# Second attention of a four-block network: the row maxima subtracted on VectorE instead of added by bf16 matmuls on TensorE

## The chip, the core and the metric

The program runs on one core of a Trainium2 chip. The metric is the device time of one execution in microseconds. The kernel before takes 2423.53 us, the median of three runs (2421.3 to 2425.45).

## What is computed

Four blocks follow each other over 2 x 1024 tokens of 256 features. The change lies in the third block's self-attention, in words "the second attention":

```python
def _attention(xq, xkv, wq, wk, wv, wo, bo):      # 16 heads of 64, both inputs are the normed x
    q = (xq @ wq).reshape(B, S, N_HEADS, D_HEAD)
    k = (xkv @ wk).reshape(B, T, N_HEADS, D_HEAD)
    v = (xkv @ wv).reshape(B, T, N_HEADS, D_HEAD)
    attn = jnp.einsum('bihd,bjhd->bhij', q, k) * D_HEAD ** (-0.5)
    attn = jax.nn.softmax(attn, axis=-1)
    out = jnp.einsum('bhij,bjhd->bihd', attn, v).reshape(B, S, D_ATTN)
    return out @ wo + bo
```

B is 2 and S and T are 1024. The softmax needs each query's largest score, which is taken off its scores before the exponential.

## The kernel before

The second attention (part_attention2, L1459 to L1838) works on 16 head pairs (PAIRS): two batches, eight pairs of heads each. TensorE, VectorE, ScalarE (ACT), GpSimd (POOL) and SP each have an instruction order written out by hand, and semaphores hold them together. Per pair there are 16 units (U): 2 halves of 512 queries times 8 blocks of 128 keys. The scores of a unit are 128 keys x 512 queries for both heads, in one of two PSUM buffers of 128x1024 (s2, named sc in the profile).

A unit n, u on TensorE (`unit`, L1594 to L1607): two bf16 matmuls (L1603) first write minus the query's maximum into the scores' buffer, from `picks`, a matrix with three rows of ones, and `shift`, which holds the negated maxima split in three bf16 parts; four fp32 matmuls (L1606; one fp32 matmul of the program appears as two instructions) then add the scores of the two heads. ScalarE takes the exponential of the whole 128x1024 from PSUM into `probs` (named pr, five buffers, KEPT; L1827). GpSimd adds the eight blocks of a half into `total` (L1686). Two units later (LAG) TensorE multiplies with the values into `o` (`values`, L1624). After each half, at units 9 and 1 of the next pair, TensorE sums `total` over the keys (`den`, L1615) into the same two buffers, ScalarE copies `o` out and inverts the sum by Ln and Exp with a table load before each (L1803, L1810, L1812), and VectorE multiplies the two (`divide`, L1738, behind the reductions of unit 3 for a pair's second half and behind unit 11's work for the first half).

The maxima of pair n+1 are found beside the units of pair n (`aside`):

- Units 0 to 2: two projections each, six in all (L1556, L1562), into `ring`, three PSUM buffers of 128x512 (ring2_, RING). ScalarE copies them out (L1791, L1796), VectorE rounds queries and keys to fp32r (L1701), two roundings each behind units 0 and 1.
- Units 3 to 10: four maxima each. TensorE computes scores of 128 queries x 512 keys in fp32r into `ring` (L1573), two before the values of that unit and two behind them; VectorE takes the row maximum of each (L1707, TENSOR_REDUCE). Maximum i waits until reduction i-3 has freed its slot.
- Unit 11: VectorE combines the halves (L1714), TensorE transposes the 16 columns of maxima (`turn`, L1578), VectorE negates and splits them in three bf16 parts (`split`, L1717 to L1731), SP writes them to DRAM (L1530) and reads them back into `shift`, three rows per head (L1536). Unit 0 of the next pair waits for it.
- Units 12 to 15 of the pairs 4, 8 and 12: two tiles of the output projection each (`project_out`, L1590), which VectorE adds to x (`add_out`, L1746).

The last pair has no successor and so only its 16 units; behind them come eight tiles of the last output projection. Before the loop, the first pair's projections, its 32 maxima and the split stand by themselves, then VectorE adds the output bias to x (`bias_out`, L1750).

Of the kernel before, what the change touches and what calls it, by code (L numbers as in the profile page):

```python
# [5 lines left out]
ALU = mybir.AluOpType  # L6
# [7 lines left out]
P = 128  # L14
# [1444 lines left out]
def part_attention2(nc, e, A):  # L1459
    with ExitStack() as ctx:  # L1460
# [14 lines left out]
        part_max, row_max = sb("pmax", [P, 2, TB, 2]), sb("rmax", [P, 2, TB])  # L1475
        top, top_rest = sb("top2", [16, P]), sb("top2_rest", [16, P])
        top_parts = [sb(f"top2_parts{i}", [16, 3, P], BF16) for i in two]
        shift = [sb(f"shift{i}", [P, T], BF16) for i in two]
        picks = sb("picks", [P, P], BF16)
# [4 lines left out]
        rows_set, shift_set = sem("rows_set2"), sem("shift_set")  # L1484
# [3 lines left out]
        top_out, shift_in = sem("top_out2"), sem("shift_in")  # L1488
        s2_made, s2_free, pv_made, sums = sem("s2m"), sem("s2f"), sem("pvm"), sem("sums")
        raw_made, rden_made, a_made, wo_made, wo_added = sem("rawm"), sem("rdenm"), sem("am"), sem("wo_made"), sem("wo_added")  # L1490
        logs = sem("logm")
        head = (slice(0, 64), slice(64, P))
# [25 lines left out]
        @block.sync  # L1518
        def _(sp):
            for i in range(1, CHUNKS):  # L1520
                for tile, src in attention2_loads(A, w[i], i):
                    sp.dma_start(tile, src).then_inc(w_in[i], 16)
            sp.dma_start(wo_w[:], A["L2_xattn_sa_wo"].rearrange("(k p) c -> p k c", p=P)).then_inc(wo_in, 16)
            sp.dma_start(wo_brep[:], A["L2_xattn_sa_bo"].partition_broadcast(P)).then_inc(wo_in, 16)
            for n, (tile, src) in enumerate(context2_loads(A, e.ctx_w0, 0)):
                sp.dma_start(tile, src).then_inc(e.ctx_w0_in[min(n, 1)], 16)
            sp.wait_ge(shift_set, 2)
            for n in range(PAIRS):
                sp.wait_ge(top_made, 5 * (n + 1))
                sp.dma_start(e.top_dram[n % 2, :, 0:16].rearrange("s r q -> r s q"), top_parts[n % 2][:]  # L1530
                             ).then_inc(top_out, 16)
                sp.wait_ge(top_out, 16 * (n + 1))
                if n >= 2:
                    sp.wait_ge(s2_made, order_of(n - 2, U - 1) + 1)
                for j in two:
                    sp.dma_start(shift[n % 2][64 * j:64 * j + 3], e.top_dram[n % 2, :, 8 * j:8 * j + 8].rearrange(  # L1536
                        "s t q -> s (t q)")).then_inc(shift_in, 16)

        @block.tensor
        def _(te):  # L1540

            def project(n, i):
# [5 lines left out]
                if i == 2 and n:  # L1548
                    te.wait_ge(top_made, 5 * (n - 1) + 1)
                if i >= RING:  # L1550
# [30 lines left out]
            def project_out(group, t):  # L1581
# [10 lines left out]
                ins.then_inc(wo_made, 1)  # L1592

            def unit(n, u):  # L1594
                half, kt = divmod(u, 8)
                at = order_of(n, u)
                if u == 0:
                    te.wait_ge(shift_in, 32 * (n + 1))
                if at >= 2:
                    te.wait_ge(s2_free, at - 1)  # L1600
                keys = slice(kt * P, (kt + 1) * P)
                for j in two:
                    te.matmul(s2[at % 2][:, j], picks[head[j]], shift[n % 2][head[j], halves[half]], start=True,  # L1603
                              stop=False)
                for j in two:
                    ins = te.matmul(s2[at % 2][:, j], kf[n % 2][head[j], keys], qf[n % 2][head[j], halves[half]],  # L1606
                                    start=False, stop=True)  # L1607
                ins.then_inc(s2_made, 1)

            def den(n, h):  # L1610
                at = den_order(n, h)
                te.wait_ge(s2_free, at - 1)
                te.wait_ge(sums, 7 * (2 * n + h + 1))
                for j in two:
                    ins = te.matmul(s2[at % 2][64 * j:64 * j + 64, 0], e.ones[:], total[h][:, j], start=True, stop=True)  # L1615
                ins.then_inc(s2_made, 1)

            def values(n, u):
                half, kt = divmod(u, 8)
                te.wait_ge(s2_free, order_of(n, u) + 1)  # L1620
                if kt == 0 and (n or half):
# [20 lines left out]
            turn(0)  # L1642
            te.wait_ge(rows_set, 2)
            te.wait_ge(shift_set, 2)
            for n in range(PAIRS):
# [23 lines left out]
        def _(pool):  # L1669
            for h in two:  # L1670
                pool.memset(shift[h][:], 0.0).then_inc(shift_set, 1)
            for n in range(PAIRS):
                for u in range(U):
# [3 lines left out]
                    at, count = U * n + u, 7 * (2 * n + half) + kt - 1  # L1677
                    pool.wait_ge(s2_free, order_of(n, u) + 1)
                    if kt == 1:
# [10 lines left out]
        def _(dve):  # L1690
            dve.memset(picks[:], 0.0).then_inc(rows_set, 1)
            dve.wait_ge(rows_set, 1)
            for j in two:
                ins = dve.memset(picks[64 * j:64 * j + 3], 1.0)
            ins.then_inc(rows_set, 1)

            def rounding(n, i):
# [18 lines left out]

            def split(n):  # L1717
                parts = top_parts[n % 2]
                dve.wait_ge(max_turned, n + 1)
                dve.tensor_scalar(top[:], ring[2][0:16, 0:P], -1.0, None, ALU.mult).then_inc(top_made, 1)  # L1720
                dve.wait_ge(top_made, 5 * n + 1)
                if n >= 2:
                    dve.wait_ge(top_out, 16 * (n - 1))
                dve.tensor_copy(parts[:, 0, :], top[:]).then_inc(top_made, 1)
                dve.wait_ge(top_made, 5 * n + 2)
                dve.tensor_tensor(out=top_rest[:], in0=top[:], in1=parts[:, 0, :], op=ALU.subtract).then_inc(top_made, 1)
                dve.wait_ge(top_made, 5 * n + 3)
                dve.tensor_copy(parts[:, 1, :], top_rest[:]).then_inc(top_made, 1)
                dve.wait_ge(top_made, 5 * n + 4)
                dve.tensor_tensor(out=parts[:, 2, :], in0=top_rest[:], in1=parts[:, 1, :],  # L1730
                                  op=ALU.subtract).then_inc(top_made, 1)  # L1731

# [25 lines left out]
            finish_maxima(0)  # L1758
            split(0)
            bias_out()  # L1760
            for n in range(PAIRS):
                for u in range(U):
                    if n + 1 < PAIRS:
                        steps, tops, turned = aside(u)
# [5 lines left out]
                        if turned:  # L1770
                            finish_maxima(n + 1)
                            split(n + 1)
                    if u == 8 + DEN_AT + 2:
# [10 lines left out]
        def _(act):  # L1784
# [20 lines left out]
            def invert(n, h):  # L1805
                at = den_order(n, h)
                act.wait_ge(s2_made, at + 1)
                if n:
                    act.wait_ge(a_made, 2 * (n - 1) + h + 1)
                act.activation(rden[h][:], s2[at % 2][:, 0], ACT.Ln).then_inc(s2_free, 1)  # L1810
                act.wait_ge(s2_free, at + 1)
                act.activation(rden[h][:], rden[h][:], ACT.Exp, scale=-1.0).then_inc(rden_made, 1)  # L1812
# [3 lines left out]
            for n in range(PAIRS):  # L1816
                for u in range(U):
                    at, here = order_of(n, u), U * n + u
                    act.wait_ge(s2_made, at + 1)
                    if here >= KEPT:  # L1820
                        act.wait_ge(pv_made, here - KEPT + 1)
                        half, kt = divmod((here - KEPT) % U, 8)
                        if kt:
                            act.wait_ge(sums, 7 * (2 * ((here - KEPT) // U) + half) + kt)
                        else:
                            act.wait_ge(sums, 7 * (2 * ((here - KEPT) // U) + half) + 1)
                    act.activation(probs[here % KEPT][:], s2[at % 2][:], ACT.Exp).then_inc(s2_free, 1)  # L1827
                    if n + 1 < PAIRS:
# [421 lines left out]
def program(nc, A, out):  # L2250
    with ExitStack() as ctx:
# [19 lines left out]
        e.mask_dram = nc.dram_tensor("mask_dram", [B, 4, T], BF16).ap()  # L2271
        e.qk_dram = nc.dram_tensor("qk_dram", [2, 8, 3, 64, T], BF16).ap()
        e.top_dram = nc.dram_tensor("top_dram", [2, 3, 32, P], BF16).ap()

# [52 lines left out]
```

## Time and profile before

| | |
|---|---|
| median of three runs | 2423.53 us |
| the profiled execution: its own time | 2423.61 us |
| the profiled execution: its span | 2421.9 us |
| mean granted TensorE clock | 0.949 of full speed |
| busy share over the span: TensorE, VectorE, ScalarE, GpSimd | 89%, 48%, 38%, 32% |
| the loop of the second attention, first to last unit | 980.5 to 1863.1 us |
| a regular pair (pair 1, from unit 12 to unit 12) | 53.5 us |

In the profile PE is TensorE's matmuls, PEld its weight loads, DVE VectorE, ACT ScalarE, POOL GpSimd, SPq SP's queue. Matmuls are pipelined: a row's duration reaches to the modelled end of the last one, so the start of the next row, not the end of the last, tells how long TensorE was taken. "x4 2.61" in a timeline is a group of four instructions that took 2.61 us from the first's start to the last's end. In square brackets stands the idle time of the engine ahead of a group and what ended it. A row of windows has the stretch, its length, the busy time of PE, PEld, DVE, ACT and POOL with their instruction counts, the granted TensorE clock, the DMA share and GB/s.

### The profile page before, as it was taken

To read this page: it belongs to the slowest core of one execution; us is meant where nothing else is said; L and a number is where in the kernel's file an instruction comes from. 1 tells how busy PE (TensorE), PEld (TensorE's weight loads), DVE (VectorE), ACT (ScalarE), POOL (GpSimd) and SP (SyncE) were. 2 spreads that over 40 slices of the span, in tenths; PEclk is the share of its full clock that TensorE was granted. 3 is DMA by queue.
4 is the path that set the end of the run, shared out by engine and by line. 5 is a ranking of instruction groups with operands and counts; after the bars stand their busy time and mean duration, and the time that the engine had idled before them with its cause. 6 is when DMAs were issued, how large, how long until landed. Compare 5 with 4: busy or idle time off the path is not lost. (4 is left out here: it accounts for less than half of the span.)

```text
span 2421.9 us, 27503 instructions
## 1 busy us (share of the span) xinstructions
PE 2144.0 (89%) x10628; PEld 1241.5 (51%) x10666; DVE 1166.1 (48%) x2077; ACT 929.9 (38%) x1413; POOL 777.5 (32%) x505
## 2 busy tenths in 40 slices
PE   5389998679889895999999999999998979898987
PEld 2234444357768683333444444333532858576766
DVE  4786662343343525645454554555451142635343
ACT  3146665223232232355535544455355321221211
POOL 3311100012131302466555664666467010202011
PEclk9699999889999996899999999999999989998989
DMA  3733420400000004000000000000000420000000
GB/s 109 110 38 40 54 29 2 109 0 1 1 1 0 1 1 119 2 1 1 1 1 1 1 1 1 1 1 1 1 1 1 121 64 1 9 1 9 0 9 9
DMA packets 48027, 51.73 MB, mean 21 GB/s; under 512 B 14618, under 2 KB 38940, under 8 KB 47620
## 3 DMA queue, kind: packets, MB, share of 16 engines
q1 hardware_dynamic: 47908, 50.12, 9.9%
q8 instruction: 77, 1.26, 0.2%
q14 instruction: 42, 0.34, 0.1%
HBM read 41.31 MB, written 8.80 MB: 21 GB/s over the span
## 5 line engine op out<-in xcount | busy, mean ns | idle before, releaser
L1686 POOL TENSOR_TENSOR total<-total,pr 128x1024 f32<-128x1024 f32 x192 | 465.0, 2422 | 242.2 <-ACT pr L1827 228.9
L1827 ACT ACTIVATE pr<-sc 128x1024 f32<-128x1024 f32 x256 | 259.7, 1021 | 355.4 <-PE sc L1606 355.4
L1707 DVE TENSOR_REDUCE pmax<-ring 128x1 f32<-128x512 f32 x512 | 325.8, 684 | 133.7 <-PE ring L1573 125.1
L1624 PE MATMUL o<-pr,v_pair 128*64 128x512 f32 x1024 | 275.7, 617 | 1.2
L1606 PE MATMUL sc<-q_full,k_full 64*128 64x512 f32 x1024 | 267.1, 591 | 0.0
L495 ACT ACTIVATE probs<-s 128x512 f32<-128x512 f32 (+1 forms) x304 | 163.2, 575 | 160.5 <-PE s L405 117.5
L1048 POOL TENSOR_TENSOR c_scores<-c_scores,c_total 128x1024 f32<-128x1024 f32 (+1 forms) x48 | 77.0, 1614 | 352.3 <-DVE c_total L1004 352.3
L1573 PE MATMUL ring<-k_round,q_round 64*128 64x512 f32 x512 | 185.2, 600 | 4.8 <-DVE pmax L1707 4.3
L973 PE MATMUL c_ps<-vw,c_pT 128*128 128x256 f32 x640 | 165.3, 418 | 22.2 <-ACT c_pT L1037 22.2
L973 PEld LDWEIGHTS c_ps<-vw,c_pT 128*128 128x128 f32 x640 | 132.2, 212 | 47.5 <-ACT c_pT L1037 25.4
L1573 PEld LDWEIGHTS ring<-k_round,q_round 64*128 64x128 f32 x512 | 74.8, 189 | 154.8 <-DVE pmax L1707 96.8
L458 DVE TENSOR_REDUCE row_max<-s 128x1 f32<-128x640 f32 (+3 forms) x128 | 126.8, 1020 | 42.7 <-PE s L387 42.3
L384 PE MATMUL s<-k_stack,q_stack 128*128 128x512 bf16 (+3 forms) x370 | 98.5, 342 | 45.3 <-DMA k_stack<-mask_dram 31.8
L923 ACT ACTIVATE c_hT<-c_ps,c_ln_b,c_ln_g 128x256 f32<-128x256 f32 x64 | 32.6, 560 | 270.1 <-PE c_ps L908 270.1
L939 PE MATMUL c_ps<-m,c_hT 128*128 128x512 f32 x256 | 121.3, 620 | 6.6 <-ACT c_hT L923 4.6
L1624 PEld LDWEIGHTS o<-pr,v_pair 128*64 128x64 f32 x1024 | 51.2, 134 | 144.2 <-issue 142.1
L1686 POOL TENSOR_TENSOR total<-pr 128x1024 f32<-128x1024 f32 x32 | 75.2, 2350 | 143.5 <-ACT pr L1827 143.5
L2121 PE MATMUL c_ps<-c_hT,hT 128*128 128x256 f32 x512 | 117.3, 392 | 4.4 <-ACT c_hT L923 4.4
L2121 PEld LDWEIGHTS c_ps<-c_hT,hT 128*128 128x128 f32 x512 | 100.2, 197 | 19.7 <-ACT c_hT L923 5.4
L1603 PE MATMUL sc<-shift,picks 64*128 64x512 bf16 x512 | 104.7, 387 | 4.8 <-DMA shift<-top_dram 4.8
L852 POOL TENSOR_TENSOR c_rstd<-c_moments,eps 128x2 f32<-128x2 f32 x48 | 9.4, 195 | 308.8 <-DVE c_moments L836 308.8
L1606 PEld LDWEIGHTS sc<-q_full,k_full 64*128 64x128 f32 x1024 | 104.5, 192 | 7.0
(278 smaller groups left out, 3407.0 us busy)
## 6 DMA issues: line engine op xcount, KB each, us to landing
qk_dram<-qk_parts SPq DMA_DIRECT2D x32, 192.0 KB, 2.8
q_stack<-qk_dram SPq DMA_DIRECT2D x48, 128.0 KB
k_stack<-qk_dram SPq DMA_DIRECT2D x48, 128.0 KB
x<-in_x SPq DMA_DIRECT2D x1, 2048.0 KB, 8.3
mlp_w<-in_L_xattn_mlp_w SPq DMA_DIRECT2D x2, 1024.0 KB, 8.4
wq<-in_L_xattn_Wq SPq DMA_DIRECT2D x2, 1024.0 KB, 6.7
wo<-in_L_xattn_Wo SPq DMA_DIRECT2D x2, 1024.0 KB, 14.9
hT<-in_L_xattn_ff_w SPq DMA_DIRECT2D x1, 2048.0 KB, 19.1
```

The source lines that it names most:

```text
L458: dve.tensor_reduce(row_max[:, heads[0], t:t + 1], src[:, 0:(t + 1) * P], AX.X, ALU.max).then_inc(s1_free, 1)
L495: act.activation(probs[at % KEPT][:, heads[0]:heads[-1] + 1, 0:width], s2[u % RING][:, 0:len(heads) * width].rearrange("p (j q) -> p j q", ...
L939: ins = te.matmul(dst, lhs[s][:, k, t * P:(t + 1) * P], m[:, s, k, c0:c0 + 512], start=k == 0, stop=k == KC - 1 and bias is None)
L973: ins = te.matmul(dst, ch.pT[s][:, c, t * P:(t + 1) * P], vw[:, s, c, :], start=c == 0, stop=c == cols // P - 1 and out_bias is None)
L1573: te.matmul(ring[i % RING][:], qr[head[j], t * P:(t + 1) * P], kr[head[j], halves[half]], start=True, stop=True).then_inc(s1_made, 1)
L1603: te.matmul(s2[at % 2][:, j], picks[head[j]], shift[n % 2][head[j], halves[half]], start=True, stop=False)
L1606: ins = te.matmul(s2[at % 2][:, j], kf[n % 2][head[j], keys], qf[n % 2][head[j], halves[half]], start=False, stop=True)
L1624: ins = te.matmul(o[64 * j:64 * j + 64], v[n % 2][:, kt, 64 * j:64 * j + 64], probs[(U * n + u) % KEPT][:, j], start=kt == 0, stop=kt == T ...
L1686: pool.tensor_tensor(out=total[half][:], in0=other[:], in1=probs[at % KEPT][:], op=ALU.add).then_inc(sums, 1)
L1707: dve.tensor_reduce(part_max[:, j, t, half:half + 1], ring[i % RING][:], AX.X, ALU.max).then_inc(s1_free, 1)
L1827: act.activation(probs[here % KEPT][:], s2[at % 2][:], ACT.Exp).then_inc(s2_free, 1)
L2121: ins = te.matmul(ch.ps[s][:, 1024 * part + 256 * f:1024 * part + 256 * (f + 1)], w.f1[:, k, chunk * P:(chunk + 1) * P], ch.hT[s][:, k, :] ...
```

## The change

VectorE now subtracts the maxima on the way out of PSUM, and TensorE adds nothing to the scores:

- The maxima stay fp32 and positive: one copy of 16x128 from PSUM (`keep_top`) takes the place of the five instructions of `split`.
- SP writes them to `level_dram` (8 KB), and one transfer sends all 8 KB to each of the 128 partitions (`level`, 128x2048 fp32, two buffers). It waits until the subtractions of the pair two before have ended.
- `unit` loses both bf16 matmuls and its wait for `shift`. It waits, as `den` does, for the step two before in the same buffers: the subtraction of a unit, or the Ln of a denominator.
- `less` is new, one per unit, 256 in all: scores (PSUM) minus `level` (SBUF) into `probs`, 128x1024 fp32. It stands first in a unit's work on VectorE, ahead of the unit's reductions and roundings, and takes over the wait for a free `probs` buffer. At unit 0 it also waits for `level`.
- The exponential runs in place in `probs`, from SBUF. GpSimd and the values wait for it by a semaphore of its own.
- `picks`, `shift` and their memsets are gone.

```diff
-            sp.wait_ge(shift_set, 2)
             for n in range(PAIRS):
-                sp.wait_ge(top_made, 5 * (n + 1))
-                sp.dma_start(e.top_dram[n % 2, :, 0:16].rearrange("s r q -> r s q"), top_parts[n % 2][:]
-                             ).then_inc(top_out, 16)
+                sp.wait_ge(top_made, n + 1)
+                sp.dma_start(e.level_dram[n % 2], top[n % 2][:]).then_inc(top_out, 16)
                 sp.wait_ge(top_out, 16 * (n + 1))
                 if n >= 2:
-                    sp.wait_ge(s2_made, order_of(n - 2, U - 1) + 1)
-                for j in two:
-                    sp.dma_start(shift[n % 2][64 * j:64 * j + 3], e.top_dram[n % 2, :, 8 * j:8 * j + 8].rearrange(
-                        "s t q -> s (t q)")).then_inc(shift_in, 16)
+                    sp.wait_ge(less_made, U * (n - 1))
+                sp.dma_start(level[n % 2][:].rearrange("p j t -> p (j t)"), e.level_dram[n % 2].rearrange(
+                    "r q -> (r q)").partition_broadcast(P)).then_inc(level_in, 16)
...
+            def slot_free(at):
+                if at >= 2:
+                    kind, n, i = turns[at - 2]
+                    if kind == "unit":
+                        te.wait_ge(less_made, U * n + i + 1)
+                    else:
+                        te.wait_ge(logs_made, 2 * n + i + 1)
+
             def unit(n, u):
                 half, kt = divmod(u, 8)
                 at = order_of(n, u)
-                if u == 0:
-                    te.wait_ge(shift_in, 32 * (n + 1))
-                if at >= 2:
-                    te.wait_ge(s2_free, at - 1)
+                slot_free(at)
                 keys = slice(kt * P, (kt + 1) * P)
                 for j in two:
-                    te.matmul(s2[at % 2][:, j], picks[head[j]], shift[n % 2][head[j], halves[half]], start=True,
-                              stop=False)
-                for j in two:
                     ins = te.matmul(s2[at % 2][:, j], kf[n % 2][head[j], keys], qf[n % 2][head[j], halves[half]],
-                                    start=False, stop=True)
+                                    start=True, stop=True)
                 ins.then_inc(s2_made, 1)
...
-            def split(n):
-                parts = top_parts[n % 2]
+            def keep_top(n):
                 dve.wait_ge(max_turned, n + 1)
...
+                dve.tensor_copy(top[n % 2][:], ring[2][0:16, 0:P]).then_inc(top_made, 1)
+
+            def less(n, u):
+                half, kt = divmod(u, 8)
+                here = U * n + u
+                dve.wait_ge(s2_made, order_of(n, u) + 1)
+                if u == 0:
+                    dve.wait_ge(level_in, 16 * (n + 1))
+                if here >= KEPT:
+                    dve.wait_ge(pv_made, here - KEPT + 1)
+                    old_half, old_kt = divmod((here - KEPT) % U, 8)
+                    dve.wait_ge(sums, 7 * (2 * ((here - KEPT) // U) + old_half) + max(old_kt, 1))
+                dve.tensor_tensor(out=probs[here % KEPT][:], in0=s2[order_of(n, u) % 2][:],
+                                  in1=level[n % 2][:, :, halves[half]], op=ALU.subtract).then_inc(less_made, 1)
...
             for n in range(PAIRS):
                 for u in range(U):
+                    less(n, u)
                     if n + 1 < PAIRS:
                         steps, tops, turned = aside(u)
...
-                    act.activation(probs[here % KEPT][:], s2[at % 2][:], ACT.Exp).then_inc(s2_free, 1)
+                    act.wait_ge(less_made, here + 1)
+                    act.activation(probs[here % KEPT][:], probs[here % KEPT][:], ACT.Exp).then_inc(exp_made, 1)
```

## Rows read from the trace of the kernel before

**Rows 1.** The page, part 1: busy time, share of the span, instructions.
```profile
PE 2144.0 (89%) x10628; PEld 1241.5 (51%) x10666; DVE 1166.1 (48%) x2077; ACT 929.9 (38%) x1413; POOL 777.5 (32%) x505
```
**Rows 2.** Windows of pair 1: units 3 to 12, then 12 to 3.
```profile
1051.07:1077.20 26.13, 25.82 (x128) 10.21 (x128) 21.61 (x34) 14.15 (x16) 17.27 (x8) 1.00 0.00 1
1077.20:1104.58 27.38, 27.29 (x125) 11.01 (x125) 7.76 (x10) 13.93 (x18) 16.58 (x8) 1.00 0.01 1
```
**Rows 3.** Timeline of TensorE in unit 6: start us, us, engine, line, what.
```profile
1060.16 0.40 PE L1603 MATMUL sc<-shift,picks 64*128 64x512 bf16 x2
1060.38 1.03 PE L1606 MATMUL sc<-q_full,k_full 64*128 64x512 f32 x4
...
1061.57 1.08 PE L1624 MATMUL o<-pr,v_pair 128*64 128x512 f32 x4
1062.58 0.49 PE L1573 MATMUL ring<-k_round,q_round 64*128 64x512 f32 x2
1062.91 0.39 PE L1603 MATMUL sc<-shift,picks 64*128 64x512 bf16 x2
```
**Rows 4.** Timeline of VectorE in the same pair: units 4 to 6, and unit 11.
```profile
1055.23 1.17 DVE L1738 TENSOR_TENSOR aT<-raw,rden 128x512 f32<-128x512 f32 x1
1056.33 3.68 DVE L1707 TENSOR_REDUCE pmax<-ring 128x1 f32<-128x512 f32 x6
...
1060.35 2.61 DVE L1707 TENSOR_REDUCE pmax<-ring 128x1 f32<-128x512 f32 x4 [0.34 <-PE ring L1573]
...
1076.32 0.17 DVE L1714 TENSOR_TENSOR rmax<-pmax 128x16 f32<-128x16 f32 x1
```
**Rows 5.** Timeline of TensorE: the transpose, unit 12, and the starts of units 14 and 15.
```profile
1076.99 0.28 PE L1578 MATMUL ring<-ident,rmax 128*16 128x128 f32 x1
1077.20 0.39 PE L1603 MATMUL sc<-shift,picks 64*128 64x512 bf16 x2
...
1081.58 0.39 PE L1603 MATMUL sc<-shift,picks 64*128 64x512 bf16 x2
...
1083.77 0.39 PE L1603 MATMUL sc<-shift,picks 64*128 64x512 bf16 x2
```
**Rows 6.** Timeline of VectorE before the loop: the first pair's maxima.
```profile
955.84 19.22 DVE L1707 TENSOR_REDUCE pmax<-ring 128x1 f32<-128x512 f32 x32 [2.94 <-PE ring L1573]
```
**Rows 7.** VectorE in a cross attention (timeline), and ScalarE's exponential from SBUF (groups).
```profile
500.60 1.22 DVE L1014 TENSOR_TENSOR c_scores<-c_ps,c_top 128x1024 f32<-128x1024 f32 x1
501.74 1.21 DVE L1001 TENSOR_REDUCE c_total<-c_scores 128x16 f32<-128x1024 f32 x1
...
L1034 ACT ACTIVATE c_scores<-c_scores 128x1024 f32<-128x1024 f32 x32 | 33.8, 1057 | 110.0 <-DVE c_scores L1014 110.0
```
**Rows 8.** Two lines of VectorE: duration in ns, min/median/max, first and last start.
```profile
L1738 DVE TENSOR_TENSOR aT<-raw,rden x32: 671/692/1177, 1028.2 to 1875.3; 128x512 f32<-128x512 f32 x32
...
L1746 DVE TENSOR_TENSOR x<-ring,x x32: 405/424/426, 1242.8 to 1891.9; 128x256 f32<-128x256 f32 x32
```
**Rows 9.** Timeline of GpSimd in the last pair.
```profile
1855.77 14.80 POOL L1686 TENSOR_TENSOR total<-total,pr 128x1024 f32<-128x1024 f32 x6 [2.49 <-ACT pr L1827]
```
**Rows 10.** Timeline of the loop's start.
```profile
977.07 4.41 DVE L1750 TENSOR_TENSOR x<-x,wo_brep 128x4096 f32<-128x4096 f32 x1
...
978.62 0.57 SPq L1536 DMA_DIRECT2D shift<-top_dram  x2
...
980.51 0.61 PE L1603 MATMUL sc<-shift,picks 64*128 64x512 bf16 x2 [4.81 <-DMA shift<-top_dram]
```
**Rows 11.** DMA issues: destination<-source, count, KB each, median us to landing.
```profile
mlp_w<-in_L_xattn_mlp_w SPq DMA_DIRECT2D x2, 1024.0 KB, 8.4
...
r_o_g<-in_L_xattn_g_out SPq DMA_DIRECT2D x1, 128.0 KB, 2.9
```
**Rows 12.** Windows before the loop, and in the first attention (columns as in rows 2).
```profile
959.00:963.00 4.00, 4.00 (x8) 1.96 (x7) 4.00 (x7) 0.00 (x0) 0.00 (x0) 0.50 1.04 214
...
145.00:150.00 5.00, 5.00 (x49) 2.87 (x47) 4.00 (x6) 3.84 (x9) 0.00 (x0) 1.00 0.02 3
```

More of the change, by code:

```diff
@@ L1475, in part_attention2 @@
         part_max, row_max = sb("pmax", [P, 2, TB, 2]), sb("rmax", [P, 2, TB])
[L1476 to L1479, printed above, removed]
+        top = [sb(f"top2_{i}", [16, P]) for i in two]
+        level = [sb(f"level{i}", [P, 2, T]) for i in two]
         ring = [ctx.enter_context(nc.psum_tensor(f"ring2_{i}", [P, 512], F32)) for i in range(RING)]
@@ L1487, in part_attention2 @@
             sem(n) for n in ("s1m", "s1f", "max_made2", "max_turned2", "top_made2"))
-        top_out, shift_in = sem("top_out2"), sem("shift_in")
-        s2_made, s2_free, pv_made, sums = sem("s2m"), sem("s2f"), sem("pvm"), sem("sums")
+        top_out, level_in = sem("top_out2"), sem("level_in")
+        s2_made, less_made, exp_made, logs_made, pv_made, sums = (
+            sem(n) for n in ("s2m", "less_made2", "exp_made2", "logs_made2", "pvm", "sums"))
         raw_made, rden_made, a_made, wo_made, wo_added = sem("rawm"), sem("rdenm"), sem("am"), sem("wo_made"), sem("wo_added")
-        logs = sem("logm")
         head = (slice(0, 64), slice(64, P))
@@ L1548, in project @@
                 if i == 2 and n:
-                    te.wait_ge(top_made, 5 * (n - 1) + 1)
+                    te.wait_ge(top_made, n)
                 if i >= RING:
@@ L1611, in den @@
                 at = den_order(n, h)
-                te.wait_ge(s2_free, at - 1)
+                slot_free(at)
                 te.wait_ge(sums, 7 * (2 * n + h + 1))
@@ L1619, in values @@
                 half, kt = divmod(u, 8)
-                te.wait_ge(s2_free, order_of(n, u) + 1)
+                te.wait_ge(exp_made, U * n + u + 1)
                 if kt == 0 and (n or half):
@@ L1669, in _ @@
         def _(pool):
-            for h in two:
-                pool.memset(shift[h][:], 0.0).then_inc(shift_set, 1)
             for n in range(PAIRS):
@@ L1690, in _ @@
         def _(dve):
[L1691 to L1695, printed above, removed]
             def rounding(n, i):
@@ L1758, in _ @@
             finish_maxima(0)
-            split(0)
+            keep_top(0)
             bias_out()
@@ L1771, in _ @@
                             finish_maxima(n + 1)
-                            split(n + 1)
+                            keep_top(n + 1)
                     if u == 8 + DEN_AT + 2:
@@ L1809, in invert @@
                     act.wait_ge(a_made, 2 * (n - 1) + h + 1)
[L1810 to L1811 removed]
+                act.activation(rden[h][:], s2[at % 2][:, 0], ACT.Ln).then_inc(logs_made, 1)
+                act.wait_ge(logs_made, 2 * n + h + 1)
                 act.activation(rden[h][:], rden[h][:], ACT.Exp, scale=-1.0).then_inc(rden_made, 1)
@@ L1817, in _ @@
                 for u in range(U):
[L1818 to L1826, printed above, removed]
-                    act.activation(probs[here % KEPT][:], s2[at % 2][:], ACT.Exp).then_inc(s2_free, 1)
+                    here = U * n + u
+                    act.wait_ge(less_made, here + 1)
+                    act.activation(probs[here % KEPT][:], probs[here % KEPT][:], ACT.Exp).then_inc(exp_made, 1)
                     if n + 1 < PAIRS:
```

16 lines of the change are left out of this document (2 added, 14 removed).

## The prediction

> **What bounds the kernel now.** I read the page's busy shares first, then windows over one head pair of the second attention, then the timelines of TensorE and VectorE inside it. On the page TensorE is busy 89% and VectorE 48% [rows 1], which looks like room for 256 new VectorE instructions; the share is a mean, so the reader should go on to the stretches. A regular pair takes 53.5 us and has two parts [rows 2]. From unit 3 to unit 12 (26.13 us, the "maxima part": eight units that carry four maxima each, then unit 11) VectorE is busy 21.61 us. From unit 12 to the next unit 3 (27.38 us, the "open part") it is busy 7.76 us. TensorE is full in both.
>
> Inside the maxima part one unit takes 1062.91 - 1060.16 = 2.75 us on TensorE, without a gap: 0.22 us from the first picks matmul to the first score matmul, 1.19 to the values, 1.01 to the last two maxima, 0.33 to the next unit [rows 3]. VectorE does four reductions in 2.61 us beside it [rows 4]. A unit of the open part that has no projection or output takes 2.19 us [rows 5]. So TensorE bounds both parts today, but in the maxima part VectorE is close behind.
>
> **How long a VectorE instruction really holds its engine.** The recorded durations overlap. Before the loop 32 reductions ran back to back in 19.22 us [rows 6]: (19.22 - 0.68)/31 = 0.598 us from start to start, while one lasts 0.68. In the loop six took 3.68 us [rows 4], again 0.60 apart. For a 128x1024 subtraction from PSUM with one operand in SBUF, the very shape of the new instruction, the trace has the cross attention's: it lasts 1.22 us and the next instruction starts 1.14 us after it [rows 7]. I take 0.60 and 1.14, which are nearest, and keep 0.68 and 1.22 as the upper end.
>
> The Trainium skill ("VectorE: DVE Perf Modes", section The DRAIN you can't avoid) says that the next instruction starts only when the pipe has emptied. Read as whole recorded durations, that gives the sum of the second case below; the rows show starts before the recorded end.
>
> **Removed: the picks matmuls.** Two per unit, 0.22 us per unit on TensorE [rows 3], 256 units: 57 us of TensorE time. This is a gain only where TensorE stays the bound. In the open part of a regular pair 7 units (12 to 15, 0 to 2) save 7 x 0.22 = 1.57 us, for 14 crossings from one pair to the next: -22 us. In the maxima part it buys nothing if VectorE is later, which is next.
>
> **Added: one subtraction per unit on VectorE, ahead of that unit's reductions.** Maxima part: 4 x 0.60 + 1.14 = 3.54 us of VectorE per unit, against 2.75 - 0.22 = 2.53 us on TensorE. The buffers don't let VectorE's work move elsewhere: the maxima have three PSUM slots, the scores two, so TensorE runs at most three reductions ahead. Is the loop longer than VectorE's own work? The fourth maximum of a unit waits for the unit's first reduction (1.14 + 0.68 = 1.82), starts some 0.06 later, the next scores 0.33 behind it, and they are there 1.08 us after (1.02 in [rows 3] and a handover): 3.3 us, before VectorE wants them at 3.54. Slack is 0.2 us. At unit 9 the denominator's matmuls use it up; I add 0.2.
>
> The part then runs: 1.1 us for unit 3's scores, 8 x 3.54 = 28.3, the division that lies at unit 3, 0.85 (1.17 there, less when GpSimd is quiet [rows 4, 8]), 0.2 at unit 9; then unit 11's subtraction, 1.14, which stands ahead of the combining of the maxima, 0.2, and the transpose, 0.21 until unit 12 [rows 4, 5] with 0.1 of handovers. Sum 32.1 against 26.13: +6.0 us. Fifteen pairs have this part (the last has no successor), the first without a division: +89 us.
>
> **Moved: the exponential now follows the subtraction.** Scores, subtraction (1.22), exponential (1.06 from SBUF [rows 7], 1.02 from PSUM today) must end before the values of two units later. In the shortest unit, 2.19 - 0.22 = 1.97 us, the values come two units and the scores' own 0.86 us (1.19 less the 0.33 of two maxima [rows 3]) after the scores' start, at 4.8 us; the chain ends at 1.1 + 1.3 + 1.1 = 3.5. Costs nothing; cover 1.3 us. On VectorE the subtraction of unit 1 stands behind the two roundings of the queries, and those behind ScalarE's copies of the projections; the order ends less than a us after today's exponential, while the values are a projection away. Nothing.
>
> **Removed: the split in three bf16 parts.** Its casts wait for GpSimd (see the division below), some 4 us per pair on VectorE, but in the open part, where VectorE has 19 us idle [rows 2]. Worth nothing in itself; GpSimd loses a disturbance.
>
> **The transfers.** Instead of two 6 KB writes SP sends the 8 KB of maxima to all 128 partitions: 1 MB. No transfer of this form is in the trace; a 128 KB broadcast landed after 2.9 us, a 1 MB load after 8.4 [rows 11]. I take 7.5 us (bounds 2.9 and, eight times a small one, 23). It is issued about 1.9 us after unit 12 and lands at 9.4; the next pair's first subtraction could run at 4 x 1.97 + 1.1 = 9.0. The 0.4 us is hidden, because TensorE has two projections next and the first thing that waits is unit 2's scores; some 3 us more would be hidden too. SP has nothing else queued there, and the buffer it writes was last read a pair earlier.
>
> **Start and end.** Today the first scores start at 980.51, held by the transfer, while VectorE adds the bias from 977.07 [rows 10]. Afterwards the scores start at once, 4.9 us earlier, but the first subtraction waits for the 1 MB, about 985. Between nothing and -5: -2.5. In the last pair the denominators wait for GpSimd, whose adds are 14.80/6 = 2.47 us apart [rows 9], more than a unit's 1.97; it starts relatively earlier, I take -2 for the whole.
>
> **Sum:** +89 - 22 - 2.5 - 2 = +62.5 us on the profiled execution's 2423.6 us, which is within 0.1 us of the median of 2423.5: 2486.
>
> **The rivals.**
> Full durations: VectorE pays 4 x 0.68 + 1.22 = 3.94 us per unit, 0.40 more, x 120 units = +48: 2533. Against it speak [rows 4, 6, 7]; for it, that no row has a reduction directly before such a subtraction with its three waits. 13%.
> Late broadcast: if it takes over some 11 us, each further us is paid at 11 crossings (the three with the output projection have 14 us more). At 15 us: +44, 2529. 3%.
> The shared path of VectorE and GpSimd: the division with both operands in SBUF lasts 671 to 1177 ns, the add with one in PSUM 405 to 426, beside the same GpSimd work [rows 8]. The new instruction is of the second kind. Were it of the first, it would wait about 0.8 us (GpSimd is busy two thirds of the part, half of a 2.4 us add left) x 120 = +96: 2581. 3%.
> TensorE's clock: at 959 to 963 us, with one 64-row maximum per 0.60 us, the granted clock was 0.50 (1.2 GHz), while at 145 to 150 it was 1.00 (2.4 GHz) [rows 12]. If the waits for VectorE brought it down in the maxima part, a unit's 2.53 us of TensorE would become 5.1 and exceed 3.54: +1.5 x 120, 2665 at most. With 2.53 of 3.54 us filled I hold it unlikely, 5%. The Trainium skill ("TensorE: Matmul & The Clock Gate", section What's actually happening) has the gate follow how busy the engine has been, which is why I keep this case.
> The other side: TensorE stays the bound. Added up over a pair, VectorE has 21.61 + 7.76 + 16 x 1.14 - 4 = 43.6 us of 53.5, so if its work could spread over the pair, all 57 us would be saved: 2366. This decides from 2.75 us per maxima unit downwards; the three slots speak against it. 5%. A mixture in which part spreads out, 2440 to 2460: 3%.
>
> **How the numbers follow.** Forecast 68%, its own range 2468 to 2503 (0.1 us more or less in a unit is 12 us, the start 3, the last pair 2). The range also takes in the full durations and the late broadcast, and most of the mixture: 2455 to 2536. About 0.2% is what a measurement of this kernel can tell from no change. Faster 0.05, same 0.02 (a cancelling mixture), slower 0.93.
>
> **What would show it.** Right: subtractions of 1.22 us, x256, followed after 1.14; units 3 to 10 at 3.5 to 3.6 us, the reductions of one unit 0.60 apart with no idle time; the maxima part near 32 us with VectorE full and TensorE waiting for its pmax; the open part 25.8 us; granted clock 1.00. Wrong: a unit near 3.9 (full durations), subtractions of over 1.3 us or of many lengths (the shared path), VectorE waiting for the level transfer (late broadcast), a clock under 1.00, or a pair under 53.5 us.

## The result, and the profile after it

The changed kernel takes 2547.5 us, the median of four runs, against 2422.4 before (the three runs of before and a fourth): the ratio is 1.0514, with a 95% interval of 1.049 to 1.054. The forecast was 2486 with a range of 2455 to 2536. The side was right, the size was half of what came: +125 us instead of +62.5. The profiled execution has a span of 2544.0 us, 122.1 more than before.

The page of the changed kernel, part 1, then the group of the new subtraction and the new transfer:

```profile
PE 2178.6 (86%) x10116; PEld 1237.8 (49%) x10154; DVE 1455.9 (57%) x2266; ACT 937.5 (37%) x1413; POOL 763.7 (30%) x503
...
L1722 DVE TENSOR_TENSOR pr<-sc,level 128x1024 f32<-128x1024 f32 x256 | 311.1, 1218 | 129.2 <-PE sc L1604 121.2
...
level<-level_dram SPq DMA_DIRECT2D x16, 1024.0 KB, 4.7
```

The shares look harmless again: VectorE went from 48% to 57% [rows 1]. The subtraction lasts 1.22 us, as in [rows 7], and the 1 MB transfer lands after 4.7 us. What answers to [rows 2] is the window of a regular pair, unit 3 to unit 12 (the maxima part) and unit 12 to the next unit 3 (the open part); columns as there:

```profile
1114.48:1149.31 34.83, 28.75 (x110) 10.72 (x109) 33.06 (x43) 14.52 (x16) 18.97 (x9) 0.95 0.00 1
1149.31:1175.96 26.65, 26.44 (x110) 10.33 (x109) 14.83 (x13) 14.08 (x17) 14.04 (x7) 1.00 0.11 40
```

The maxima part grew from 26.13 to 34.83 us, with VectorE busy 33.06 of them; the open part shrank from 27.38 to 26.65. Forecast were 32.1 and 25.8. So both terms were missed, in the same direction: 2.7 and 0.8 us per pair. The timeline of VectorE in that maxima part shows where (start us, us, engine, line, what; in brackets idle time ahead):

```profile
1116.80 2.48 DVE L1695 TENSOR_REDUCE pmax<-ring 128x1 f32<-128x512 f32 x4
1119.19 1.77 DVE L1730 TENSOR_TENSOR aT<-raw,rden 128x512 f32<-128x512 f32 x1
1120.88 1.21 DVE L1722 TENSOR_TENSOR pr<-sc,level 128x1024 f32<-128x1024 f32 x1
1122.01 2.47 DVE L1695 TENSOR_REDUCE pmax<-ring 128x1 f32<-128x512 f32 x4
1124.40 1.21 DVE L1722 TENSOR_TENSOR pr<-sc,level 128x1024 f32<-128x1024 f32 x1
...
1127.03 1.29 DVE L1695 TENSOR_REDUCE pmax<-ring 128x1 f32<-128x512 f32 x2 [0.22 <-PE ring L1568]
1128.43 1.23 DVE L1722 TENSOR_TENSOR pr<-sc,level 128x1024 f32<-128x1024 f32 x1
1129.57 2.48 DVE L1695 TENSOR_REDUCE pmax<-ring 128x1 f32<-128x512 f32 x4
1131.96 1.22 DVE L1722 TENSOR_TENSOR pr<-sc,level 128x1024 f32<-128x1024 f32 x1
...
1146.10 1.22 DVE L1722 TENSOR_TENSOR pr<-sc,level 128x1024 f32<-128x1024 f32 x1
1147.23 1.82 DVE L1702 TENSOR_TENSOR rmax<-pmax 128x16 f32<-128x16 f32 x1
1149.42 0.28 DVE L1709 COPY top<-ring 16x128 f32<-16x128 f32 x1 [0.37 <-PE ring L1573]
1149.63 2.42 DVE L1730 TENSOR_TENSOR aT<-raw,rden 128x512 f32<-128x512 f32 x1
```

From one subtraction to the next it is 3.52 to 3.53 us (1124.40 - 1120.88, 1131.96 - 1128.43): the forecast's 3.54, without a gap. What is longer stands between: the division at 1119.19 holds VectorE for 1.69 us instead of 0.85; one unit takes 4.03 us (1124.40 to 1128.43); and the combining of the maxima, 128x16, lasts 1.82 us at 1147.23, where it lasted 0.17 before [rows 4]. GpSimd's timeline at the same time:

```profile
1118.05 2.36 POOL L1680 TENSOR_TENSOR total<-total,pr 128x1024 f32<-128x1024 f32 x1 [1.25 <-ACT pr L1813]
...
1146.67 4.83 POOL L1680 TENSOR_TENSOR total<-total,pr 128x1024 f32<-128x1024 f32 x2 [2.92 <-ACT pr L1813]
```

An add that began at 1118.05 ends at 1120.41, and the division is done 0.55 us later; the first of the two adds from 1146.67 ends about 1149.03, if it takes 2.36 us as the others do, and the combining ends at 1149.05. That both waited for GpSimd is here only read off the times; the second and third experiment test it. Over the whole trace the two instructions, both with two operands in SBUF, read (ns, min/median/max):

```profile
L1702 DVE TENSOR_TENSOR rmax<-pmax x16: 178/1814/1826, 975.5 to 1934.6; 128x16 f32<-128x16 f32 x16
...
L1730 DVE TENSOR_TENSOR aT<-raw,rden x32: 682/1980/2431, 1026.6 to 1997.2; 128x512 f32<-128x512 f32 x32
```

The 0.51 us by which the unit of 1124.40 is longer has another source. TensorE had waited 2.08 us for the reductions behind the division, and then its clock fell. Timeline of TensorE, then windows around it:

```profile
1122.74 0.50 PE L1568 MATMUL ring<-k_round,q_round 64*128 64x512 f32 x1 [2.08 <-DVE pmax L1695]
...
1124.36 1.91 PE L1622 MATMUL o<-pr,v_pair 128*64 128x512 f32 x4
```
```profile
1117.50:1122.70 5.20, 3.13 (x12) 1.23 (x12) 5.20 (x7) 1.05 (x2) 2.36 (x1) 1.00 0.00 0
...
1124.40:1127.70 3.30, 3.30 (x10) 1.19 (x11) 3.08 (x6) 1.06 (x1) 2.13 (x2) 0.51 0.00 0
```

The values took 1.91 instead of 1.08 us, at a granted clock of 0.51, which is the 1.2 GHz level. The Trainium skill ("TensorE: Matmul & The Clock Gate", section What's actually happening) lets the clock follow how busy the engine has been; here it fell behind the wait. It does not fall behind every such wait: the division is this long in all 14 pairs that have it there, and the clock fell behind it in 12 of them. TensorE's wait for the combining, 2.3 us in each of 15 pairs, brought it down in four (pairs 5, 6, 13 and 14); behind the first three the open part took 28.3 us instead of 26.65. Timeline of TensorE at the transpose of pair 3, where the clock stayed, and of pair 5, where it fell, then the open part of pair 5:

```profile
1210.56 0.28 PE L1573 MATMUL ring<-ident,rmax 128*16 128x128 f32 x1 [2.29 <-DVE rmax L1702]
...
1348.28 0.28 PE L1573 MATMUL ring<-ident,rmax 128*16 128x128 f32 x1 [2.30 <-DVE rmax L1702]
...
1351.29 2.04 PE L1604 MATMUL sc<-q_full,k_full 64*128 64x512 f32 x4
```
```profile
1348.49:1376.78 28.29, 28.08 (x109) 10.53 (x109) 13.16 (x13) 14.08 (x17) 14.04 (x7) 0.94 0.11 38
```

### The profile page after: what moved, and what is told of

The parts are those of the page before. It is cut to its first block and busy times, and to the rows that moved or that the text cites. A ratio compares the mean times of both kernels' runs of the same rounds, so it can differ in the third digit from the quotient of the medians.

```text
span 2544.0 us, 26649 instructions
## 1 busy us (share of the span) xinstructions
PE 2178.6 (86%) x10116; PEld 1237.8 (49%) x10154; DVE 1455.9 (57%) x2266; ACT 937.5 (37%) x1413; POOL 763.7 (30%) x503
## 5 line engine op out<-in xcount | busy, mean ns | idle before, releaser
L1680 POOL TENSOR_TENSOR total<-total,pr 128x1024 f32<-128x1024 f32 x192 | 452.9, 2359 | 341.3 <-ACT pr L1813 332.6
L1813 ACT ACTIVATE pr<-pr 128x1024 f32<-128x1024 f32 x256 | 269.9, 1055 | 519.4 <-DVE pr L1722 518.7
L1722 DVE TENSOR_TENSOR pr<-sc,level 128x1024 f32<-128x1024 f32 x256 | 311.1, 1218 | 129.2 <-PE sc L1604 121.2
L1695 DVE TENSOR_REDUCE pmax<-ring 128x1 f32<-128x512 f32 x512 | 317.9, 680 | 6.9 <-PE ring L1568 6.9
L1604 PE MATMUL sc<-q_full,k_full 64*128 64x512 f32 x1024 | 319.1, 648 | 0.0
L1568 PE MATMUL ring<-k_round,q_round 64*128 64x512 f32 x512 | 253.6, 610 | 58.1 <-DVE pmax L1695 57.2
L1622 PE MATMUL o<-pr,v_pair 128*64 128x512 f32 x1024 | 289.2, 644 | 3.5 <-ACT raw L1796 2.9
L1568 PEld LDWEIGHTS ring<-k_round,q_round 64*128 64x128 f32 x512 | 91.1, 196 | 258.8 <-DVE pmax L1695 165.6
```

Of the source, the lines that this page charges most:

```text
L1568: te.matmul(ring[i % RING][:], qr[head[j], t * P:(t + 1) * P], kr[head[j], halves[half]], start=True, stop=True).then_inc(s1_made, 1)
L1622: ins = te.matmul(o[64 * j:64 * j + 64], v[n % 2][:, kt, 64 * j:64 * j + 64], probs[(U * n + u) % KEPT][:, j], start=kt == 0, stop=kt == T ...
L1680: pool.tensor_tensor(out=total[half][:], in0=other[:], in1=probs[at % KEPT][:], op=ALU.add).then_inc(sums, 1)
L1695: dve.tensor_reduce(part_max[:, j, t, half:half + 1], ring[i % RING][:], AX.X, ALU.max).then_inc(s1_free, 1)
L1722: dve.tensor_tensor(out=probs[here % KEPT][:], in0=s2[order_of(n, u) % 2][:], in1=level[n % 2][:, :, halves[half]], op=ALU.subtract).then_ ...
L1813: act.activation(probs[here % KEPT][:], probs[here % KEPT][:], ACT.Exp).then_inc(exp_made, 1)
```

## The experiments

Each ratio is against the kernel before, on the same chip. The experiments ran on three chips, on which the kernel before took 2423.3 to 2424.6 us, so a difference between two experiments can be off by about 1 us. Theory A throughout: VectorE bounds the maxima part and only that; what the forecast missed is the wait of two-operand instructions for GpSimd, the clock behind it, and a removal that is worth less than the matmuls' spacing.

**The removal alone.** Leaves out the subtraction of the maxima:

```diff
-                for j in two:
-                    te.matmul(s2[at % 2][:, j], picks[head[j]], shift[n % 2][head[j], halves[half]], start=True,
-                              stop=False)
```

> The kernel before without the two picks matmuls of a unit: the maxima are found and sent, but not taken off the scores (this part of the computation is left out). It prices the removal alone. Theory A (from the trace after, where a unit without picks takes 2.07 us instead of 2.19): the score's first weight load comes out from under the picks matmul, the removal is worth 0.12 us per unit, 256 units, about -25 to -31 us, 2391 to 2398. Theory B (my prediction's 0.22 per unit, with VectorE's 2.4 us still below the unit's 2.53): -55 us, 2368.

Measured: 2405.0 us, ratio 0.992 (0.990 to 0.994), -19 us. Even less than theory A's -25 to -31. Windows of one pair, maxima part and open part, and TensorE's timeline in a maxima unit:

```profile
1099.86:1125.43 25.57, 25.08 (x111) 9.31 (x110) 21.26 (x34) 13.88 (x16) 17.20 (x8) 1.00 0.00 1
1125.43:1152.08 26.65, 26.44 (x110) 10.34 (x109) 8.78 (x10) 14.20 (x18) 16.84 (x8) 1.00 0.00 1
```
```profile
1108.82 1.02 PE L1603 MATMUL sc<-q_full,k_full 64*128 64x512 f32 x4
...
1110.19 1.08 PE L1621 MATMUL o<-pr,v_pair 128*64 128x512 f32 x4
1111.20 0.51 PE L1573 MATMUL ring<-k_round,q_round 64*128 64x512 f32 x2
1111.54 1.03 PE L1603 MATMUL sc<-q_full,k_full 64*128 64x512 f32 x4
```

A maxima unit takes 2.72 us instead of 2.75 (1111.54 - 1108.82): the picks are gone, but from the first score matmul to the values it is 1.37 us instead of 1.19 [rows 3]. In an open unit it is 2.07 instead of 2.19. So 57 us of matmul starts were worth 19 us of time. That the fp32 weight loads had lain under the picks matmuls is my reading of it. It fits the traces: in the open unit of 1081.58 in [rows 5] they begin with the picks, 0.22 us ahead of the first score matmul, and in the changed kernel they begin together with it. But no run tests it; the runs show the sizes, not the cause.

**GpSimd's adds cut to 16 columns.** Leaves out most of the denominator (`total` is filled with ones once, ahead of the loop):

```diff
-                    pool.tensor_tensor(out=total[half][:], in0=other[:], in1=probs[at % KEPT][:],
-                                       op=ALU.add).then_inc(sums, 1)
+                    pool.tensor_tensor(out=total[half][:, :, 0:8], in0=other[:, :, 0:8],
+                                       in1=probs[at % KEPT][:, :, 0:8], op=ALU.add).then_inc(sums, 1)
```

> The changed kernel with GpSimd's adds cut from 1024 to 16 columns (most of the softmax denominator is left out). Theory A (combining the maxima and the division, both with two operands in SBUF, wait for GpSimd's running add): the combining at unit 11 falls from 1.8 to 0.18 us, the divisions from about 2.0 to 0.68, the maxima part of a pair from 34.8 to 31.5 to 32 us; 15 x 3 = -45 us, and the last pair's denominators wait no longer, about -10 more: 2485 to 2497. Theory B (the extra time is in longer chains of handovers between scores, subtraction and exponential): the durations fall only if they are GpSimd's, and the maxima part stays at 34 to 35 us; only the last pair gains, 2537.

Measured: 2482.9 us, ratio 1.025 (1.023 to 1.026), 65 us less than the changed kernel. The same two instructions (now L1705 and L1733):

```profile
L1705 DVE TENSOR_TENSOR rmax<-pmax x16: 159/161/174, 973.8 to 1881.2; 128x16 f32<-128x16 f32 x16
...
L1733 DVE TENSOR_TENSOR aT<-raw,rden x32: 668/678/693, 1023.2 to 1933.6; 128x512 f32<-128x512 f32 x32
```

No long one is left. The waits were for GpSimd. Of the 65 us, 48 lie in the maxima parts (added up over the 15 pairs of both traces) and 5 in the three open parts in which the clock had fallen; in this trace the clock is 1.00 in these places.

**The maxima combined by a reduction**, which reads one tensor:

```diff
-                dve.tensor_tensor(out=row_max[:], in0=part_max[:, :, :, 0], in1=part_max[:, :, :, 1],
-                                  op=ALU.max).then_inc(max_made, 1)
+                dve.tensor_reduce(row_max[:], part_max[:], AX.X, ALU.max).then_inc(max_made, 1)
```

> The changed kernel with one instruction replaced: the two halves' maxima are combined by a reduction over one tensor instead of a maximum of two, so that it has one operand in SBUF. Theory A (it waits for GpSimd because of its second SBUF operand): it lasts about 0.2 us instead of 1.8, the transpose and unit 12 come 1.6 us earlier, 15 x 1.6 = -24 us, 2523. Theory B (it is the position behind the subtraction, or a wait for its own engine, that makes it long): no change, 2547.

Measured: 2515.7 us, ratio 1.038 (1.036 to 1.040), -32 us, with GpSimd's adds at full size:

```profile
L1702 DVE TENSOR_REDUCE rmax<-pmax x16: 171/172/188, 974.3 to 1905.6; 128x16 f32<-128x32 f32 x16
```

Timelines of VectorE and of GpSimd at the same place in this trace, then GpSimd in the kernel before:

```profile
1083.58 0.17 DVE L1702 TENSOR_REDUCE rmax<-pmax 128x16 f32<-128x32 f32 x1
...
1083.02 2.35 POOL L1680 TENSOR_TENSOR total<-total,pr 128x1024 f32<-128x1024 f32 x1 [2.92 <-ACT pr L1812]
```
```profile
1076.40 4.96 POOL L1686 TENSOR_TENSOR total<-total,pr 128x1024 f32<-128x1024 f32 x2 [3.21 <-ACT pr L1827]
```

GpSimd's add begins 0.56 us ahead of the reduction here, and as far ahead of the long maximum in the changed kernel (1146.67 and 1147.23). In the kernel before it began 0.08 us behind the maximum of 1076.32 [rows 4]. So the 0.17 us of before hung on a start that was just early enough.

The instruction is short, as theory A has it. Of the -32 us its 15 x 1.65 explain 25: added up over both traces, the maxima parts are 25.1 us shorter. Another 5.0 come from the open parts of pairs 5, 6 and 13, which take 26.64 us now: the long wait for the combining is gone, and the clock stays up there. Some 2 us are left, the size of the noise.

**And the division of unit 3 ahead of that unit's subtraction**, on top of it:

```diff
                 for u in range(U):
+                    if u == DEN_AT + 2 and n:
+                        divide(n - 1, 1)
                     less(n, u)
...
-                    if u == DEN_AT + 2 and n:
-                        divide(n - 1, 1)
```

> As the third kernel, and the division of the pair's second half moved ahead of unit 3's subtraction, where VectorE is idle and the inverse is ready. Theory A: the division no longer stands between the reductions of unit 3 and unit 4, the maxima part loses the 1.7 us it takes there and the 0.5 us stall behind it, 14 x 2 = -28 us more, 2495. Theory B (VectorE would be late there anyway, since unit 3's scores are what it waits for, or the division is locked for long at the new place too): -10 us or less more.

Measured: 2484.0 us, ratio 1.025 (1.023 to 1.026), another -32 us. Windows of one pair, and VectorE's timeline at units 3 and 4:

```profile
1109.91:1140.89 30.98, 27.71 (x111) 10.40 (x110) 29.54 (x42) 13.79 (x16) 17.50 (x8) 1.00 0.00 1
1140.89:1167.53 26.64, 26.43 (x109) 10.34 (x108) 13.88 (x14) 14.81 (x18) 15.82 (x8) 1.00 0.11 40
```
```profile
1108.87 0.69 DVE L1729 TENSOR_TENSOR aT<-raw,rden 128x512 f32<-128x512 f32 x1 [2.68 <-ACT rden L1804]
1111.09 1.23 DVE L1721 TENSOR_TENSOR pr<-sc,level 128x1024 f32<-128x1024 f32 x1 [1.52 <-PE sc L1604]
1112.23 2.47 DVE L1695 TENSOR_REDUCE pmax<-ring 128x1 f32<-128x512 f32 x4
1114.62 1.22 DVE L1721 TENSOR_TENSOR pr<-sc,level 128x1024 f32<-128x1024 f32 x1
```

The clock is 1.00 in both parts now: the long wait of TensorE went with the long division. This kernel is what the forecast described, and it takes what the forecast said, though by two errors that cancel in part: the division costs nothing here (the sum had 0.85), and the removal gives less.

**A further reduction of 0.60 us per unit, in the maxima part or in the open part**, 120 each, on top of the fourth kernel:

```diff
+                if 3 <= u < 11 and n + 1 < PAIRS:
+                    dve.tensor_reduce(spare[:, here % 16:here % 16 + 1], s2[order_of(n, u) % 2][:, 0], AX.X,
+                                      ALU.max)
```
The other has the condition `(u < 3 or u >= 11) and n + 1 < PAIRS`.

> As the fourth kernel, with one more reduction of 128x512 from PSUM on VectorE (0.60 us) ahead of the subtraction in units 3 to 10, 120 in all. Theory A (VectorE's own time bounds these units and nothing else does): all of it is paid, 120 x 0.60 = +72 us on 2484, 2556; the unit is 4.12 us instead of 3.52. Theory B (the units are bound by the circle through TensorE and ScalarE, and VectorE has room inside it): less than +40.

> As the fourth kernel, with the same extra reduction in units 0 to 2 and 11 to 15 instead, again 120 in all. Theory A: only unit 11's stands before the transpose and is paid, 15 x 0.6 = +9 us, the others lie in VectorE's idle time: 2490 to 2496. Theory B (the handovers score, subtraction, exponential, values are on the path everywhere): near +72, 2550.

Measured: 2553.3 us (+69.3) and 2492.7 us (+8.7) against 2484.0. The same work costs 0.58 us per instruction in one part and 0.07 in the other, where the 15 ahead of the transpose explain all of it (15 x 0.6 = 9). This is the decisive pair: VectorE's own time bounds the maxima part, and the handovers through the exponential are covered in the open part.

**The maxima spread over more units.** Three kernels on top of the fourth, in the 12 pairs without output projection: over units 3 to 15; over units 3 to 12; and over 3 to 15 with the first half's division behind the transpose, as the second has it too.

```diff
+            return steps, range(S1 * (u - 3) // 13, S1 * (u - 2) // 13) if u >= 3 else (), u == 15
...
+            return steps, range(S1 * (u - 3) // 10, S1 * (u - 2) // 10) if 3 <= u < 13 else (), u == 13
...
-                    if u == 8 + DEN_AT + 2:
+                    if u == (11 if n % GROUP == 0 or n + 1 == PAIRS else 15):
                         divide(n, 0)
```

> As the fourth kernel, with the same 32 maxima of a pair spread over units 3 to 15, two or three per unit, and the transpose at unit 15, in the 12 pairs without output projection. Theory A (it is the place of VectorE's work, not its amount): VectorE then has 13 subtractions and 32 reductions, 34 us, from unit 3 to the next pair against 39.2 us today, some 3 us per pair come back, 12 x 3 = -36 us, 2440 to 2460. Theory B (the sum of VectorE's work or the later transfer of the maxima bounds it): no gain, or slower, because the 1 MB transfer now lands some 7 us into the next pair.

> As the spread of the seventh kernel, but over units 3 to 12, with the transpose at unit 13 and the division of the first half behind it. Theory A (the spread lost because the division of the first half came ahead of the transpose, because TensorE's wait there brought its clock down, and because the maxima arrived late): the maxima land in time, the division is hidden, 12 x 1.5 = -18 us against the fourth kernel's 2484, 2466. Theory B (spreading gives nothing, since VectorE's total is what counts): 2484 or more.

> The seventh kernel (maxima over units 3 to 15) with the division of the first half moved behind the transpose of unit 15. Theory A: its 1.6 us no longer stand in the stretch that VectorE fills, 12 x 1.6 = -19 us on 2490, 2471, while the late maxima and the clock after the transpose stay. Theory B: no change, 2490.

Measured: 2490.3, 2467.2 and 2462.8 us. The first spread was a miss: 2440 to 2460 were expected, and it is 6 us slower than the fourth kernel. Its windows, from unit 3 to the next unit 0, from there to unit 3, and behind the transpose, then VectorE behind unit 11's reductions and at the next pair's start:

```profile
1110.62:1148.52 37.90, 34.33 (x142) 12.40 (x141) 35.98 (x47) 18.65 (x20) 29.55 (x13) 1.00 0.00 1
1148.52:1168.54 20.02, 19.81 (x77) 8.83 (x76) 7.84 (x9) 9.52 (x13) 3.81 (x3) 0.91 0.15 53
...
1150.00:1152.00 2.00, 2.00 (x5) 0.50 (x2) 0.00 (x0) 0.00 (x0) 0.00 (x0) 0.50 0.38 66
```
```profile
1135.83 1.71 DVE L1730 TENSOR_TENSOR aT<-raw,rden 128x512 f32<-128x512 f32 x1
...
1155.15 1.23 DVE L1722 TENSOR_TENSOR pr<-sc,level 128x1024 f32<-128x1024 f32 x1 [6.24 <-DMA level<-level_dram]
```

The division now stood inside the stretch that VectorE fills and waited for GpSimd, 1.71 us; and after TensorE's wait for the transpose the clock was 0.50. Moving the division alone gave 27 us where 19 were expected, and spreading to unit 12 gave 17 against the fourth kernel (18 expected). There the maxima land 1.9 to 5.1 us into unit 0 of the next pair, and TensorE's units are as long as in the fourth kernel. So the place of VectorE's work matters and not only its amount.

How much of the first spread's loss is the late transfer, and how much the clock? The third kernel has the transfer as late (it lands 6.0 to 7.5 us into unit 0) and is the fastest of the three. Its windows over unit 0 behind pair 1 and behind pair 2:

```profile
1086.27:1093.57 7.30, 7.30 (x18) 2.24 (x17) 2.09 (x3) 0.00 (x0) 3.05 (x2) 0.77 0.36 145
1142.50:1148.20 5.70, 5.70 (x17) 1.94 (x16) 0.88 (x2) 0.00 (x0) 3.06 (x2) 1.00 0.52 183
```

Unit 0 takes 5.70 us, as in the fourth kernel, where the clock stays at 1.00, and 1.6 us more where it fell. Of the 11 crossings between regular pairs the clock fell at 9 in the first spread and at 4 in the third, each time behind the same wait of 1.8 us for the transpose. The late transfer shows only where unit 0 was not long: units 1 and 2 then take 0.1 to 1.5 us more than elsewhere. So the first spread lost more to the clock than to the transfer. None of the three reaches the kernel before.

**Both ways in one kernel.** The kernel before, with the subtraction only in units 0, 1, 13, 14 and 15 of the first 15 pairs, where VectorE is idle, and picks and shift elsewhere; then the same with the second half's division ahead of unit 3's reductions; then that move alone on the kernel before.

```diff
+        LESS = (0, 1, 13, 14, 15)
+        in_place = lambda n, u: u in LESS and n + 1 < PAIRS
...
+                    if in_place(n, u):
+                        less(n, u)
```

> The kernel before, with picks and shift kept in units 2 to 12, and the subtraction on VectorE in units 0, 1, 13, 14 and 15 of the first 15 pairs, where the trace after shows it hidden. Theory A (a unit without picks is worth 0.12 us there and costs nothing): 14 x 5 x 0.12 = -8 us against before, 2415. Theory B (the splits' casts, which wait for GpSimd, or the additional transfers delay unit 13's subtraction): no change or slower than before, 2424 to 2435.

> The eighth kernel (subtraction on VectorE in units 0, 1, 13, 14 and 15, picks elsewhere), with the second half's division ahead of unit 3's reductions, where VectorE waits. Theory A: the 1.17 us division between the reductions, which costs units 3 to 5 0.8 us more than three others, is hidden, 14 x 0.8 = -11 us on 2414, 2403. Theory B (TensorE bounds those units anyway): 2414.

> The kernel before with that move alone, to part the two gains of the eleventh. Theory A: -11 us, 2412. Theory B: 2423.

Measured: 2414.1 us, ratio 0.9963 (0.9949 to 0.9977); 2401.4 us, ratio 0.9914 (0.990 to 0.993); 2414.8 us, ratio 0.9965 (0.9952 to 0.9979). Each is faster than the kernel before, by little but clear of the noise, and the second, 0.86% faster, beats both. In the second and third the maxima part of a regular pair takes 25.36 us instead of 26.13 [rows 2]. The divisions of the second, against 671 to 1177 ns in [rows 8]:

```profile
L1773 DVE TENSOR_TENSOR aT<-raw,rden x32: 671/691/693, 1023.0 to 1852.0; 128x512 f32<-128x512 f32 x32
```

## Why the prediction was half right

What bounds the kernel was right: VectorE in the maxima part, TensorE elsewhere. Three terms of the sum failed: the combining of the maxima (0.2 us), the division at unit 3 (0.85) and the picks matmuls that went (0.22 per unit). The first two were priced as if GpSimd's adds did not hold them up at their new times.

- **VectorE bounds the maxima part, 3.54 us per unit: right.** Measured 3.52, from 0.60 and 1.14 us of spacing; the full durations (3.94) are refuted. The Trainium skill ("VectorE: DVE Perf Modes", section The DRAIN you can't avoid) has the next instruction wait for the empty pipe, but also says, which the prediction left out, that one that is not held starts earlier; the rows here show such earlier starts, so its recorded durations must not be added up.
- **The combining of the maxima, "0.2": wrong, and the largest miss.** It takes 1.82 us. I priced it by the row of before, where GpSimd's add happened to begin 0.08 us behind it. It has two operands in SBUF, the kind that my own [rows 8] show waiting, and the change moved it to a moment when an add is already running. 15 x 1.65 = 25 us; the run without it gave 32, since it also spared TensorE the wait behind which its clock fell in three pairs.
- **The division at unit 3, "0.85": wrong for the same reason.** 1.69 us, then a unit 0.51 us longer because TensorE's clock fell behind the wait (in 12 of 14 pairs, by different amounts): about 14 x 1.35 = 19 us. Together with the 0.85 already in the sum, its run gave 32.
- **The picks, "0.22 us": wrong.** 0.12 in a light open unit, 0.73 us instead of 1.57 per pair: 14 x 0.84 = 12 us. I took the distance between two starts as what goes away.
- **The contention rival** looked at the subtraction alone. That was right for the subtraction, whose 256 durations stay within 1206 to 1227 ns; but the waiting fell on its neighbours.
- **The clock rival**: it did fall, but for some 3 us in most pairs, not in the whole part.
- **The transfer, 7.5 us:** it takes 4.7 and is hidden. **The start, -2.5:** unit 3 of the first pair comes at 993.7 instead of 998.4 us, -4.7. **The last pair, -2:** from its forerunner's unit 12 to the last output projection 61.3 us instead of 59.5, +1.8.
- **The exponential behind the subtraction: right**, it costs nothing in the open part, and 0.6 us more there is hidden too.

Added up over the unit starts of the two profiled executions, the 122.1 us are +130.1 in the 15 maxima parts (forecast 89), -5.2 in the 14 open parts (forecast -22), -4.7 at the start and +1.9 from unit 12 of the last pair but one to the end. The maxima parts' 41 us too much are 25 of the combining and about 19 of the division with the clock behind it, less some 3 by which the other terms had been set too high. The open parts' 17 are 12 of the picks and 5 of the three in which the clock had fallen.

That the fourth kernel took the forecast's time is in part luck, as said there. And the sums of the rivals that end in 2533, 2529, 2581 and 2665 are each 1 us low, counted from 2486; nothing rests on it.

## What to carry to other kernels

Before work is added to an engine, read the stretches and not the share, and price it by the spacing of back-to-back instructions there. Then look again at every instruction that stands near it and has two operands in SBUF beside a busy GpSimd: its old duration is a matter of timing, and the cure may be a form with one tensor operand or a place where the engine is idle. What a removed matmul gives back is seen only by removing it.

## What the runs showed of the hardware

- A VectorE maximum of 128x16 with two operands in SBUF lasts 0.17 us where GpSimd's add begins 0.07 to 0.09 us behind it, and 1.8 us where the add began 0.56 us ahead of it; the same result by a reduction lasts 0.17 us with the add as far ahead.
- The granted clock fell to 0.51 for some 3 us after a wait of TensorE of 2.08 us, though it was busy before and after. Such falls came behind 12 of 14 waits at this place of the changed kernel, behind 4 of 15 waits of 2.3 us at another, and in the first spread and its variant behind 9 and 4 of 11 waits of 1.8 us: the length of the wait alone does not tell.
- Two bf16 matmuls ahead of four fp32 ones cost 0.22 us in starts, and 0.12 us of time in an open unit, 0.03 in a maxima unit.
- An 8 KB row sent from DRAM to 128 partitions, 1 MB in all, landed after 4.6 to 4.9 us in each of the changed kernel's 16 transfers.
